# Layer 1 of a two-layer graph network in 880 groups of one chunk, with four tile numbers packed in a word

## The chip, the cores and the metric

The kernel runs on one core of one Trainium2 chip. The metric is the device time of one execution in microseconds (us); the lower the better. Each number of "before" is the median of three executions, or is read from one further execution that was taken with a profile.

## The reference, cut to what matters

There are 6250 nodes with 512 features, and 106,250 directed edges (50,000 drawn pairs in both directions and a self loop for each node), sorted by `dst`. Every layer sums over the edges of a node, divides by their number and multiplies by a weight matrix.

```python
def layer0(x, src, dst):                 # sums rows x[src] into node dst
    x_l = x @ W_l.T + b_l
    agg = segment_sum(x_l[src], dst, num_segments=6250)
    deg = segment_sum(ones, dst, num_segments=6250)
    return agg / maximum(deg, 1)[:, None] + x @ W_r.T

def layer1(h, src, dst):                 # sums rows h[dst] into node src
    neigh = segment_sum(h[dst] @ W_neigh.T + b_neigh, src, num_segments=6250)
    deg = segment_sum(ones, src, num_segments=6250)
    out = relu(h @ W_self.T + b_self + neigh / maximum(deg, 1)[:, None])
    return layernorm(h + out) * gamma + beta

x = layernorm(x + layer0(x, src, dst))
x = layernorm(x + layer1(x, src, dst))
```

## The kernel before

**Tiles, chunks, groups.** The 6250 nodes are T = 49 tiles of 128. An edge belongs to the tile of the node into which it is summed. The edges are laid out tile by tile in chunks of 128, one edge in each partition. A chunk is summed by TensorE: a gather brings the 128 table rows of its edges (1028 half-precision numbers each: high half, low half, scale), a 128x128 one-hot matrix says which node of the tile each edge goes to, and three matmuls multiply it with the high halves, the low halves and a column that counts edges. A group is a run of chunks of one tile whose matmuls accumulate in the same pair of PSUM banks. After a group, VectorE adds the 128x513 sum to `acc[:, tile, :]`. The number of groups is fixed from the worst case and not from the data, so groups that no tile needs stand at the end of the list. Positions to which no edge falls hold index 0 and a node offset that matches nothing.

**Layer 0** has 464 groups of two chunks, 928 chunks. In the same loop the edges of layer 1 are brought to their places: for each of 832 columns VectorE writes `where` (L901), a row of CHUNKS[1] positions, and TensorE multiplies it in two halves (`place`, L1178). `bin_starts` (L677) has worked out before it where each tile of a layer begins, and the tile of each group (`g_tile`, L720). It runs for layer 1 before the first table is written. Between the layers come the layer's weights and norm, 49 tiles long, in which the codes of layer 1's edges are unpacked (`decode_*`).

**Layer 1** has 464 groups of two chunks too. Its loop goes over 32 chunks at a time:

- POOL (`far_gathers`, L530) issues one indirect gather for each chunk into 16 buffers (`rows1`): eight in `rows`, five in `flat`, and one each in `g_loc`, `g_idx` and `edges`. For chunk n it waits until TensorE has done chunk n-16, and every eight chunks for the indices.
- ScalarE (`hots`, L1485) makes the one-hot matrices, four chunks at a time.
- TensorE (`row_sums`, L1262) sums the chunks into one of three pairs of PSUM banks, in the order `PAIR`, and waits until the addition that last used the pair is done. Beside the chunks it turns and multiplies one 128x512 block of h by `W_self` for every 16 chunks (`side_turn`, four transposes, and `side_product`, four fp32 matmuls), until all 49 blocks are done, after 800 chunks or so.
- VectorE (`adds`, L963) loads the group's tile number from `g_tile` into a register, waits for its own addition before, waits for the group's matmuls and adds (`add_group`, L952). It hands over indices and node offsets eight chunks at a time (`hand_batch`, L947), and for each block of h it adds two biases (`evict`, L910; `add_beta`, L915).
- SyncE moves the blocks of h and of the side products between DRAM and SBUF.

The lines of an addition are these:

```python
tile = dve.value_load(g_tile[1][0:1, ds(n, 1)], min_val=0, max_val=T - 1)
dve.wait_ge(s_acc, group0(1) + n)
dve.wait_ge(s_mm, chunk0(1) + G1 * (n + 1))
```

After the last addition come the inverse degrees and 49 tiles of projection and norms. All matmuls of a chunk have one line, 1117, since a helper issues them.

Of the kernel before, what the change touches and what calls it, by code (L numbers as in the profile page):

```python
# [18 lines left out]
def gnn_two_layers(nc, x, src, dst, w_l_t, b_l, w_r_t, w_self_t, b_self, w_neigh_t, b_neigh, gamma, beta, out):  # L19
    f32, f16, bf16, i32 = mybir.dt.float32, mybir.dt.float16, mybir.dt.bfloat16, mybir.dt.int32  # L20
    ALU, ACT, AX = mybir.AluOpType, mybir.ActivationFunctionType, mybir.AxisListType
    ds = bass.ds
# [3 lines left out]
    T = -(-N // P)  # L26
    LAST = N - (T - 1) * P
    KC = D // P
    U = 16
# [4 lines left out]

    GROUP = (2, 2)
    GROUPS = [-(-(-(-E // (P * g)) + T - 1) * g // U) * U // g for g in GROUP]

# [24 lines left out]
    with ctx:  # L62
# [69 lines left out]
        g_loc = [sb(f"g_loc{l}", [P, CHUNKS[l]], f32) for l in range(2)]  # L132
        g_tile = [sb(f"g_tile{l}", [1, CHUNKS[0]], i32) for l in range(2)]
        dst_next = g_idx[1][:, 0:EC]
        past = g_loc[1][0:T, :]
# [7 lines left out]
        row_unit = sb("row_unit", [P, 1], f32)  # L143
        PAIR = [0, 1, 2, 0, 1, 2, 0, 1]
        G1 = GROUP[1]
        assert len(PAIR) * G1 == U and CHUNKS[1] % (2 * U) == 0

# [316 lines left out]
        def _(pool):  # L464
# [34 lines left out]
            for layer in range(2):  # L499
# [29 lines left out]

                def far_gathers(i, first=False):  # L530
                    for k in range(2 * U):
                        n = 2 * U * i + k
                        if k % H == 0:
                            pool.wait_ge(s_idx, chunk0(1) // H + 2 * U // H * i + k // H + 1)
                        if not (first and k < U):
                            used = chunk0(1) + n - U + 1
                            if not isinstance(used, int):
                                used = pool.to_reg(used)
                            pool.wait_ge(s_sel, 2)
                            pool.wait_ge(s_mm, used)  # L540
                        nc.gpsimd.indirect_dma_start(  # L541
                            out=rows1[k % U], out_offset=None, in_=tables[1][:, :],
                            in_offset=bass.IndirectOffsetOnAxis(ap=idx_ring[:, k:k + 1], axis=0),
                        ).then_inc(s_row[k % U], 16)

                if layer == 0:
                    gathers(0, first=True)
                    with pool.Fori(1, CHUNKS[0] // U) as i:
                        gathers(i)
                else:  # L550
                    pool.wait_ge(s_mm, chunk0(1))
                    far_gathers(0, first=True)
                    with pool.Fori(1, CHUNKS[1] // (2 * U)) as i:
                        far_gathers(i)

            pool.wait_ge(s_deg, 2)
# [13 lines left out]
        def _(dve):  # L570
# [106 lines left out]
            def bin_starts(layer):  # L677
# [25 lines left out]
                for b in range(MB):  # L703
# [3 lines left out]
                dve.wait_ge(s["cscp"], 1)  # L707
                V.tensor_scalar(past, iota_chunk[0:T, :], cs_col[:, 0:1], None, ALU.is_ge).then_inc(s["past"], 1)
                link(V.tensor_scalar(base[:], cs_col[:], float(P * g), None, ALU.mult))
# [10 lines left out]
                V.tensor_copy(g_tile[layer][:, 0:n].rearrange("p (h c) -> p h c", h=2),  # L720
                              ps[0:1, 6:8, 0:half]).then_inc(s["list"], 1)

            def bin_rank(layer, b):
# [227 lines left out]

            def add_group(i, q):  # L952

                n = 2 * len(PAIR) * i + q
                tile = dve.value_load(g_tile[1][0:1, ds(n, 1)], min_val=0, max_val=T - 1)
                dve.wait_ge(s_acc, group0(1) + n)
# [6 lines left out]
            def adds(i, last=False, side=(None, None), beside=(None, None)):  # L963

                for q in range(2 * len(PAIR)):
                    b = G1 * q // H
                    if G1 * q % H == 0 and not (last and b >= 2):
                        hand_batch(2 * U // H * i + b + 2, (b + 2) % 4)
                    if q % len(PAIR) == 2 and beside[q // len(PAIR)] is not None:
                        add_beta(beside[q // len(PAIR)])  # L970
                    if q % len(PAIR) == len(PAIR) - 1 and side[q // len(PAIR)] is not None:
                        evict(side[q // len(PAIR)])
                    add_group(i, q)

            for layer in range(2):
# [14 lines left out]
                else:  # L990
# [8 lines left out]
                    adds(T // 2, side=(T - 2, T - 1), beside=(T - 1, None))  # L999
                    with dve.Fori(T // 2 + 1, iters // 2 - 1) as i:  # L1000
                        adds(i)
                    adds(iters // 2 - 1, last=True)
                dve.wait_ge(s_acc, group0(layer) + GROUPS[layer])
# [111 lines left out]
        def _(pe):  # L1115
# [145 lines left out]

            def row_sums(i, first=False, turn=(None, None), product=(None, None)):  # L1262
                for r in range(2):
                    for k in range(U):
# [19 lines left out]
            for layer in range(2):  # L1284
# [13 lines left out]
                else:  # L1298
# [6 lines left out]
                    with pe.Fori(T // 2 + 1, iters // 2) as i:  # L1305
                        row_sums(i)
                pe.wait_ge(s_acc, group0(layer) + GROUPS[layer])
                if layer == 1:
# [52 lines left out]
        def _(act):  # L1361
# [122 lines left out]

            def hots(i, first=False, turn=(None, None)):  # L1485
                for j in range(2 * U // HB):
                    n, at = 2 * U * i + HB * j, HB * (j % 2)
# [19 lines left out]
            with act.Fori(T // 2 + 1, CHUNKS[1] // (2 * U)) as i:  # L1507
                hots(i)
            act.wait_ge(s_lproj, 2 * T)

# [68 lines left out]
```

## Time and profile before

| | before |
|---|---|
| median of 3 executions | 3032.01 us (3031.95 to 3041.6) |
| profiled execution | 3039.64 us, its span 3037.9 us |
| from the first gather of layer 1 to its last addition's end | 1616.8 to 2808.0 us of the span |
| busy share of the span: TensorE, VectorE, ScalarE, POOL | 78%, 65%, 47%, 66% |
| mean granted TensorE clock | 0.907 of full speed |

The profiled execution is 7.6 us above the median and like the slowest of the three. Register, branch, semaphore and DMA-issuing instructions don't count as busy; an engine that is idle in the profile can be held by them.

### The profile page before, as it was taken

The page shows a single profiled execution, that of the slowest core. Times are in us where ns is not written, and L with a number is a line of the kernel's source. Part 1 is how long each engine was busy: PE and PEld are TensorE (multiplying, and loading weights), DVE is VectorE, ACT ScalarE, POOL GpSimd, SP SyncE. Part 2 cuts the span into 40 slices and gives each one's busy share as a digit, 9 for nine tenths or more (in the row PEclk, how much of TensorE's full clock was granted, in tenths as well). Part 3 has the DMA queues.
Part 4 walks back from the last instruction along what each step waited for, and adds up shares of the span by engine and source line. Part 5 has one row for each costly group of instructions (what it writes and reads, how often), then busy time and mean ns, then how long its engine had stood idle before and what let it go on. Part 6 is the DMA issues. An engine that isn't in the chain of part 4 may idle for free.

```text
span 3037.9 us, 52213 instructions
## 1 busy us (share of the span) xinstructions
PE 2376.5 (78%) x10032; PEld 1021.4 (34%) x10032; DVE 1960.0 (65%) x4549; ACT 1421.2 (47%) x3617; POOL 1998.1 (66%) x2069
## 2 busy tenths in 40 slices
PE   3288989989999988987885677776767777666996
PEld 2133434444444434433432232222323222221443
DVE  6899888888888888877873333333333333322898
ACT  3502555555565555553444443444344433431676
POOL 0276777777777777761115777777777777774785
PEclk8589999999999999999997989899888899865998
DMA  5577777777788777774557888888888888778676
GB/s 197 174 198 229 230 221 232 222 234 233 227 234 232 228 229 234 219 208 125 166 166 232 250 250 251 252 245 248 247 246 250 250 246 251 224 204 153 226 241 203
DMA packets 250848, 676.72 MB, mean 223 GB/s; under 512 B 40360, under 2 KB 41190, under 8 KB 250788
## 3 DMA queue, kind: packets, MB, share of 16 engines
q0 software_dynamic: 148480, 488.56, 57.0%
q1 hardware_dynamic: 101828, 186.19, 18.3%
q10 hardware_dynamic: 480, 1.28, 0.1%
q8 instruction: 24, 0.39, 0.1%
q14 instruction: 36, 0.29, 0.0%
HBM read 585.90 MB, written 89.97 MB: 222 GB/s over the span
## 4 chain that ended last, share of the span: by engine, by line
PE 32%; DMA 26%; DVE 17%; issue 14%; POOL 6%; DVEq 3%; ACT 1%; POOLq 1%; SPq 0%; ACTq 0%
PE ps L1117 31%; DMA rows<-table,idx_ring 13%; DMA flat<-table,idx_ring 9%; POOL rows L541 3%; DVE acc L889 2%; DVE onehot L876 2%; DVEq L883 2%; DMA table<-rows 1%; DVE where L901 1%; DMA edges<-table,idx_ring 1%; POOL flat L541 1%; POOL rows L525 1%; DVE flat L1072 1%; DVE spot L1072 1%; DVE flat L1089 1%
## 5 line engine op out<-in xcount | busy, mean ns | idle before, releaser
L1117 PE MATMUL ps<-rows,onehot 128*128 128x512 f16 x4176 | 895.3, 332 | 348.0 <-DMA rows<-table,idx_ring 172.3
L525 POOL DMA_INDIRECT rows<-table,idx_ring x928 | 895.1, 965 | 313.5 <-issue 207.5
L961 DVE TENSOR_TENSOR acc<-acc,ps 128x513 f32 x464 | 320.1, 690 | 798.2 <-PE ps L1117 795.5
L1117 PEld LDWEIGHTS ps<-rows,onehot 128*128 128x128 bf16 x4176 | 374.7, 102 | 919.3 <-issue 194.7
L541 POOL DMA_INDIRECT rows<-table,idx_ring x464 | 438.5, 945 | 158.5 <-issue 99.9
L1117 PE MATMUL ps<-where,put 128*128 128x464 bf16 x1664 | 467.9, 363 | 36.7 <-DVE where L901 28.2
L1117 PE MATMUL ps<-w_b,flat 128*128 128x512 f32 x784 | 463.4, 675 | 0.0
L901 DVE TENSOR_SCALAR where<-iota_chunk,cw_ring 128x928 bf16<-128x928 f16 x832 | 438.0, 526 | 7.5 <-PE ps L1117 0.6
L1425 ACT ACTIVATE put<-spot,flat 128x128 f16<-128x128 f16 x832 | 265.7, 390 | 338.1 <-PE ps L1117 330.7
L1413 ACT ACTIVATE spot<-iota_node,flat 128x128 f16<-128x128 f16 x832 | 340.4, 479 | 128.4 <-DVE flat L745 128.4
L889 DVE TENSOR_TENSOR acc<-acc,ps 128x513 f32 x464 | 318.1, 686 | 95.3 <-PE ps L1117 49.8
L541 POOL DMA_INDIRECT flat<-table,idx_ring x290 | 279.7, 964 | 88.3 <-issue 59.4
L876 DVE TENSOR_SCALAR onehot<-iota_node,loc_ring,rows 128x128 bf16<-128x128 f16 x928 | 311.1, 335 | 22.1 <-DMA rows<-table,idx_ring 20.4
L1493 ACT ACTIVATE apart<-iota_node,loc_ring 128x128 f16<-128x128 f16 x928 | 293.2, 387 | 6.2 <-DVE idx_ring L950 6.0
L1117 PE MATMUL ps<-w_a,flat 128*128 128x512 f32 x592 | 277.0, 612 | 5.4 <-ACT flat L1515 5.3
L1117 PE MATMUL ps<-flat,put 128*128 128x512 f16 (+1 forms) x870 | 195.1, 347 | 105.5 <-DMA flat<-table,idx_ring 95.3
L1498 ACT ACTIVATE onehot<-apart,row_unit 128x512 bf16<-128x512 f16 x116 | 83.7, 722 | 317.3 <-PE ps L1117 316.6
L1117 PEld LDWEIGHTS ps<-where,put 128*128 128x128 f16 x1664 | 121.0, 98 | 233.5 <-issue 104.2
L1117 PEld LDWEIGHTS ps<-flat,put 128*128 128x128 bf16 x870 | 77.4, 105 | 292.1 <-issue 151.9
L506 POOL COPY acc<-zeros 128x513 f32 (+1 forms) x49 | 35.2, 717 | 212.7 <-ACT flat L1450 212.7
L1483 ACT ACTIVATE flat<-ps 128x512 f32<-128x512 f32 x49 | 29.2, 597 | 306.7 <-PE ps L1117 306.7
L1117 PEld LDWEIGHTS ps<-w_a,flat 128*128 128x128 f32 x592 | 109.5, 195 | 122.3 <-issue 110.5
(233 smaller groups left out, 2450.2 us busy)
## 6 DMA issues: line engine op xcount, KB each, us to landing
table<-rows SPq DMA_DIRECT2D x98, 257.0 KB, 4.0
rows<-table,idx_ring POOLq DMA_INDIRECT x1392, 3.8
xr_scratch<-edges SPq DMA_DIRECT2D x49, 256.0 KB
rows<-xr_scratch SPq DMA_DIRECT2D x49, 256.0 KB, 3.2
h_scratch<-rows SPq DMA_DIRECT2D x49, 256.0 KB, 2.1
flat<-h_scratch SPq DMA_DIRECT2D x49, 256.0 KB
hb_scratch<-spot SPq DMA_DIRECT2D x49, 256.0 KB, 3.8
u_scratch<-flat SPq DMA_DIRECT2D x49, 256.0 KB
```

The source lines that it names most:

```text
L525: nc.gpsimd.indirect_dma_start(out=rows[:, k % GB, :], out_offset=None, in_=tables[layer][:, :], in_offset=bass.IndirectOffsetOnAxis(ap=id ...
L541: nc.gpsimd.indirect_dma_start(out=rows1[k % U], out_offset=None, in_=tables[1][:, :], in_offset=bass.IndirectOffsetOnAxis(ap=idx_ring[:, ...
L876: V.tensor_scalar(onehot[:, k % SB, :], iota_node[:], loc_ring[:, k:k + 1], rows[:, k % GB, 2 * D:2 * D + 2].bitcast(f32), ALU.is_equal, A ...
L883: tile = dve.value_load(g_tile[layer][0:1, ds(U // g * i + q, 1)], min_val=0, max_val=T - 1)
L889: V.tensor_tensor(tile_acc, tile_acc, part, ALU.add).then_inc(s_acc, 1)
L901: V.tensor_scalar(where_bf[:, k % PB, 0:CHUNKS[1]], iota_chunk[:, 0:CHUNKS[1]], cw_ring[:, k, 0:1], cw_ring[:, k, 1:2], ALU.is_equal, ALU. ...
L961: V.tensor_tensor(tile_acc, tile_acc, part, ALU.add).then_inc(s_acc, 1)
L1117: return nc.tensor.matmul(*args, skip_group_check=True, **kw)
L1413: last = nc.scalar.activation(spot[:, PB * g + k, :], iota_node[:], ACT.Abs, scale=value[:, ds(col + k, 1)], bias=shift_v[:, ds(col + k, 1)])
L1425: nc.scalar.activation((put1, put2)[g][:, k, :], spot[:, PB * g + k, :], ACT.Relu, scale=-1.0, bias=value[:, ds(col + k, 1)]).then_inc(s[" ...
L1493: last = nc.scalar.activation(apart[:, at + k, :], iota_node[:], ACT.Abs, bias=loc_ring[:, HB * j + k:HB * j + k + 1])
L1498: nc.scalar.activation(hot1[j % (U // HB)], apart[:, at:at + HB, :], ACT.Relu, bias=row_unit[:], scale=-2.0 ** -HS).then_inc(s_hot, HB)
```

## The change

Layer 1 is cut in 880 groups of one chunk (`GROUP = (2, 1)`), 880 chunks in place of 928. Layer 0 keeps its 464 groups of two. Since 880 is an odd number of 16s, every loop over 32 chunks gets a last half of 16. The order of the PSUM pairs is written out for 16 groups; it brings a pair back after three groups, and twice in 16 after two. The tile number isn't loaded for each addition: after the list of tile numbers is made, three further operations on one partition pack four 6-bit numbers in a word (`g_tiles`), VectorE loads a word for four additions, before the last addition of the four before, and splits it in registers. All that is as wide as layer 1's list becomes narrower: `where`, `past`, `place`, `decode_*`.

```diff
-    GROUP = (2, 2)
+    GROUP = (2, 1)
+        g_tiles = sb("g_tiles", [1, CHUNKS[1] // 4], i32)
-        PAIR = [0, 1, 2, 0, 1, 2, 0, 1]
+        PAIR = [0, 1, 2, 0, 1, 2, 0, 1, 2, 0, 1, 2, 0, 1, 2, 1]
-                def far_gathers(i, first=False):
-                    for k in range(2 * U):
+                def far_gathers(i, first=False, count=2 * U):
+                    for k in range(count):
...
+                    far_gathers(CHUNKS[1] // (2 * U), count=U)
...
+                if layer:
+                    dve.wait_ge(s["list"], 1)
+                    of = g_tile[1][:, 0:n].rearrange("p (c g) -> p c g", g=4)
+                    link(V.scalar_tensor_tensor(of[:, :, 0], of[:, :, 1], 64.0, of[:, :, 0], ALU.mult, ALU.add))
+                    link(V.scalar_tensor_tensor(of[:, :, 2], of[:, :, 3], 64.0, of[:, :, 2], ALU.mult, ALU.add))
+                    link(V.scalar_tensor_tensor(g_tiles[:], of[:, :, 2], 4096.0, of[:, :, 0], ALU.mult, ALU.add))
...
-            def add_group(i, q):
+            def four_tiles(i, q):
+
+                four = dve.value_load(g_tiles[0:1, ds(len(PAIR) // 2 * i + q // 4, 1)])
+                tiles = []
+                for k in range(4):
+                    one = dve.scalar_reg_alu(ALU.arith_shift_right, four, 6 * k) if k else four
+                    tiles.append(dve.snap(dve.scalar_reg_alu(ALU.bitwise_and, one, 63)).with_bounds(min_val=0, max_val=T - 1))
+                return tiles
+
+            def add_group(i, q, tile):
 
                 n = 2 * len(PAIR) * i + q
-                tile = dve.value_load(g_tile[1][0:1, ds(n, 1)], min_val=0, max_val=T - 1)
...
-                for q in range(2 * len(PAIR)):
+                count = len(PAIR) if last else 2 * len(PAIR)
+                following = four_tiles(i, 0)
+                for q in range(count):
...
-                    add_group(i, q)
+                    if q % 4 == 0:
+                        tiles = following
+                    if q % 4 == 3 and q + 1 < count:
+                        following = four_tiles(i, q + 1)
+                    add_group(i, q, tiles[q % 4])
```

## Rows read from the trace of the kernel before

**Rows 1.** The page: busy tenths of POOL, granted clock, GB/s, in 40 slices.
```profile
POOL 0276777777777777761115777777777777774785
PEclk8589999999999999999997989899888899865998
GB/s 197 174 198 229 230 221 232 222 234 233 227 234 232 228 229 234 219 208 125 166 166 232 250 250 251 252 245 248 247 246 250 250 246 251 224 204 153 226 241 203
```
**Rows 2.** Windows: busy (x instructions) PE, PEld, DVE, ACT, POOL; clock, DMA, GB/s.
```profile
1900.00:2200.00 300.00, 216.10 (x890) 86.70 (x889) 103.56 (x208) 120.05 (x310) 227.51 (x239) 0.91 0.83 248
...
2700.00:2720.00 20.00, 13.27 (x50) 4.18 (x49) 5.83 (x12) 7.78 (x20) 15.13 (x17) 0.73 0.75 210
...
2760.00:2780.00 20.00, 12.35 (x37) 3.38 (x36) 4.35 (x8) 5.78 (x15) 14.81 (x17) 0.50 0.97 158
```
**Rows 3.** Source line 541, layer 1's gathers: duration ns min/median/max, first and last start.
```profile
L541 POOL DMA_INDIRECT rows<-table,idx_ring x464: 942/946/967, 1616.8 to 2770.8; - x155
...
L541 POOL DMA_INDIRECT edges<-table,idx_ring x58: 942/946/948, 1635.6 to 2781.6; - x58
...
DMA to landing us min/median/max: 3.5/4.0/24.8
```
**Rows 4.** Timeline, the end of layer 1's edges: start, us, what, idle before.
```profile
2781.33 1.03 PE L1117 MATMUL ps<-rows,onehot 128*128 128x512 f16 x3 [0.55 <-DMA rows<-table,idx_ring]
...
2806.07 1.04 PE L1117 MATMUL ps<-edges,put 128*128 128x512 f16 x3 [0.21 <-DMA edges<-table,idx_ring]
...
2807.33 0.69 DVE L961 TENSOR_TENSOR acc<-acc,ps 128x513 f32 x1 [2.17 <-PE ps L1117]
```
**Rows 5.** Timeline of VectorE in layer 1, around a bias addition.
```profile
1646.44 0.69 DVE L961 TENSOR_TENSOR acc<-acc,ps 128x513 f32 x1 [1.64 <-PE ps L1117]
1647.05 0.69 DVE L919 TENSOR_TENSOR spot<-flat,edges 128x512 f32<-128x512 f32 x1
1647.65 0.69 DVE L961 TENSOR_TENSOR acc<-acc,ps 128x513 f32 x1
```
**Rows 6.** Waits, 400 to 1292 us: engine, line, waited for; us, times, longest.
```profile
DVE cw_ring L897 <- DVE idx_ring L853: 6.8, 38, 0.2
```
**Rows 7.** Source lines 955 and 961: the tile number's load and the addition; idle before.
```profile
L955 DVEq FUSED_REGOPS  x880: 53/190/190, 1611.5 to 2804.8; - x176
L955 DVEq TENSOR_LOAD <-g_tile x464: 299/305/970, 1611.0 to 2804.5; - x155
```
```profile
L961 DVEq FUSED_REGOPS  x464: 57/57/64, 1625.2 to 2807.2; - x155
L961 DVE TENSOR_TENSOR acc<-acc,ps x464: 679/690/692, 1625.3 to 2807.3; 128x513 f32 x155
...
  PE ps L1117: 795.5, 434
```
**Rows 8.** Timeline of TensorE in layer 1, at either clock.
```profile
2307.98 3.58 PE L1117 MATMUL ps<-rows,onehot 128*128 128x512 f16 x12 [1.37 <-DMA rows<-table,idx_ring]
...
2318.28 2.05 PE L1117 MATMUL ps<-w_b,flat 128*128 128x512 f32 x2
...
2321.74 1.10 PE L1117 MATMUL ps<-w_b,flat 128*128 128x512 f32 x2
...
2323.14 0.59 PE L1117 MATMUL ps<-g_loc,put 128*128 128x512 f16 x3
...
2323.60 0.59 PE L1117 MATMUL ps<-g_idx,put 128*128 128x512 f16 x3
```
**Rows 9.** Groups by form, 400 to 1292 us: busy us, mean ns; idle before, releasers.
```profile
L525 POOL DMA_INDIRECT rows<-table,idx_ring x692 | 669.1, 967 | 224.0 <-issue 145.5 <-PE ps L1117 78.5
...
L901 DVE TENSOR_SCALAR where<-iota_chunk,cw_ring 128x928 bf16<-128x928 f16 x691 | 363.7, 526 | 6.7 <-PE ps L1117 0.6
```
**Rows 10.** Timeline of VectorE where `g_tile` of layer 1 is written.
```profile
97.15 0.63 DVE L720 CAST g_tile<-ps 1x464 int32<-1x464 f32 x1
97.70 0.17 DVE L842 TENSOR_SCALAR top<-top 128x49 f32<-128x49 f32 x1
```

More of the change, by code:

```diff
@@ L143, in gnn_two_layers @@
         row_unit = sb("row_unit", [P, 1], f32)
-        PAIR = [0, 1, 2, 0, 1, 2, 0, 1]
+        PAIR = [0, 1, 2, 0, 1, 2, 0, 1, 2, 0, 1, 2, 0, 1, 2, 1]
         G1 = GROUP[1]
-        assert len(PAIR) * G1 == U and CHUNKS[1] % (2 * U) == 0
+        assert len(PAIR) * G1 == U and CHUNKS[1] % (2 * U) == U and CHUNKS[1] % HB == 0
         def pair_before(q):
@@ L707, in bin_starts @@
                 dve.wait_ge(s["cscp"], 1)
-                V.tensor_scalar(past, iota_chunk[0:T, :], cs_col[:, 0:1], None, ALU.is_ge).then_inc(s["past"], 1)
+                V.tensor_scalar(past, iota_chunk[0:T, 0:CHUNKS[1]], cs_col[:, 0:1], None, ALU.is_ge).then_inc(s["past"], 1)
                 link(V.tensor_scalar(base[:], cs_col[:], float(P * g), None, ALU.mult))
@@ L963, in adds @@
             def adds(i, last=False, side=(None, None), beside=(None, None)):
-                for q in range(2 * len(PAIR)):
+                count = len(PAIR) if last else 2 * len(PAIR)
+                following = four_tiles(i, 0)
+                for q in range(count):
                     b = G1 * q // H
-                    if G1 * q % H == 0 and not (last and b >= 2):
+                    if G1 * q % H == 0 and not last:
                         hand_batch(2 * U // H * i + b + 2, (b + 2) % 4)
@@ L999, in _ @@
                     adds(T // 2, side=(T - 2, T - 1), beside=(T - 1, None))
-                    with dve.Fori(T // 2 + 1, iters // 2 - 1) as i:
+                    with dve.Fori(T // 2 + 1, iters // 2) as i:
                         adds(i)
-                    adds(iters // 2 - 1, last=True)
+                    adds(iters // 2, last=True)
                 dve.wait_ge(s_acc, group0(layer) + GROUPS[layer])
@@ L1260, in sums, with row_sums @@
                         x_turn(turn, half)
-            def row_sums(i, first=False, turn=(None, None), product=(None, None)):
-                for r in range(2):
+            def row_sums(i, first=False, turn=(None, None), product=(None, None), halves=2):
+                for r in range(halves):
                     for k in range(U):
@@ L1306, in _ @@
                         row_sums(i)
+                    row_sums(iters // 2, halves=1)
                 pe.wait_ge(s_acc, group0(layer) + GROUPS[layer])
@@ L1483, in side_turned, with hots @@
                 nc.scalar.activation(h_t, ps[:, 0, :], ACT.Copy).then_inc(s_ltc, 1)
-            def hots(i, first=False, turn=(None, None)):
-                for j in range(2 * U // HB):
+            def hots(i, first=False, turn=(None, None), count=2 * U):
+                for j in range(count // HB):
                     n, at = 2 * U * i + HB * j, HB * (j % 2)
@@ L1508, in _ @@
                 hots(i)
+            hots(CHUNKS[1] // (2 * U), count=U)
             act.wait_ge(s_lproj, 2 * T)
```

## The prediction

> **What bounds the kernel now.** I read the page first, by its slices. POOL is at 7 tenths in two long stretches, one for each layer's edges, and GB/s falls from about 250 to 204 and 153 at the end of the second [rows 1]. So I asked for windows of that stretch. Between 1900 and 2200 us POOL issues 239 gathers in 300 us, one each 1.255 us, at 248 GB/s, with VectorE busy 104 of 300 us and TensorE 216 [rows 2]. The source view of the gathers gives the same pace over nearly the whole stage: chunk 0 starts at 1616.8 and chunk 919, the last in `rows`, at 2770.8, so (2770.8 - 1616.8) / 919 = 1.2557 us per chunk; a gather lasts 0.946 us of it and the other 0.31 is POOL's own issue [rows 3]. VectorE's idle time before its additions is 795.5 us, 434 times for the matmuls [rows 7]: it follows. The stage is therefore POOL's instruction count times 1.2557 us, up to a point.
>
> That point shows in the last rows. After about 2720 us POOL goes on at its pace, but 210 GB/s become 158 while the DMA engines' share rises from 0.75 to 0.97 [rows 2], and the time to landing, 4.0 us in the median, ends at 24.8 us [rows 3]. TensorE then takes a chunk when its rows land: 15 chunks from 2781.33 to 2806.07 are 24.74 / 15 = 1.65 us each, and the last addition starts at 2807.33 and ends at 2808.0 [rows 4]. What is special there? I counted the edge list of the reference: with ceilings per tile, groups of 256 edges need 440 groups, that is 880 chunks. Chunk 880 is issued at 1616.8 + 880 x 1.2557 = 2721.8 us, where the rate falls. The 48 chunks behind it are padding; every lane has index 0, so all 128 rows are the same table row. I take it that they are slow because of that; the trace shows the time and place only.
>
> **The change, part by part.** Its time is summed against the profiled execution, 3039.6 us.
>
> *Fewer chunks in layer 1.* With groups of 128 the same count gives 854 chunks with edges, and 880 in all, so 26 of padding. Chunks with edges: 880 - 854 = 26 fewer at POOL's 1.2557 us, -32.6 us. Padding: 48 - 26 = 22 fewer at 1.65 us, -36.3 us. Together -68.9. This supposes that POOL stays what paces the stage, so the rest is whether VectorE and TensorE keep below 16 x 1.2557 = 20.1 us in 16 chunks.
>
> *VectorE.* It has 16 additions in 16 chunks where it had 8. One is 0.690 us [rows 7]. Each waits for the one before. How long from its end to the next one's start, when all else is ready? No addition in the trace shows it well. The nearest row is a copy that waits for its predecessor, then for a second semaphore, then has its register operations: 6.8 us in 38 times, 0.18 us [rows 6]; the upper bound I take is 0.25, the same with a 0.057 us register step more [rows 7]. So 16 x 0.87 = 13.9 us (15.0 at most). A bias addition behind an addition delays the next one by little: three starts 0.61 and 0.60 us apart [rows 5], against 0.87 without it, so 2 x 0.35 = 0.7 (2 x 0.75 at most). Handing over, 0.3 to 0.5. Splitting a word happens four times: the load is 0.305 us, the register work for its address up to 0.190, and seven shifts and masks with four copies cost between one fused step at 0.190 and eleven at 0.057, 0.63 [rows 7]; with gaps 0.8 to 1.3 us. It is issued while the addition before runs, which covers 0.69. So 0.1 to 0.6 is exposed, and all 1.3 if nothing is covered; I take 0.4, in all 1.6. The sum is 13.9 + 0.7 + 0.4 + 1.6 = 16.6 us of 20.1, and the upper bound 15.0 + 1.5 + 0.5 + 5.2 = 22.2. The two are far apart; I take the lower because row 5 shows an addition starting 0.6 us behind another operation with its whole load of a tile number between them, so register work is indeed covered.
>
> *TensorE.* At the high clock a chunk is 0.46 us (2323.14 to 2323.60) and at the low one 3.58 / 4 = 0.895; a side matmul is 1.10 or 2.05 [rows 8]. With four of these in 16 chunks that is 7.4 + 4.4 = 11.8 us or 14.3 + 8.2 = 22.5. At the present mean clock of 0.91 [rows 2], 18% of the time at the low level, it is about 13.7 of 20.1. Its waits for additions change: a pair of banks held two chunks, now one, so it can be three chunks ahead of VectorE and not six. A chunk needs the addition three before: 0.87 + 0.87 us lie between, more than a chunk at either clock, and less than a side matmul and a chunk at the low one (2.95). The 16 gather buffers stand between such stalls and POOL: a row lands after some 5 chunks, which leaves about 11, or 13 us. I add 4 us for stalls that come through (0 to 18).
>
> *Do more additions slow POOL?* In layer 0 a gather has a mean of 0.967 us beside a busy VectorE, in layer 1 a median of 0.946 [rows 3, 9]. If the denser additions did what layer 0's work does, it would be 880 x 0.021 = 18 us; I take 0, because the long ones stand out in the layer that has `where`, and an addition reads PSUM in both. The Trainium skill, "SBUF — State Buffer", section "SBUF: two separate sides", says the same of the mechanism: only an operation in a two-port mode keeps GpSimd from writing descriptors, and a later section there says that `tensor_tensor` has no such mode. By that rule the term is 0, by the bound from layer 0 it is +18.
>
> *Layer 0.* `where` is 928 wide at 0.526 us [rows 9] and becomes 880: 5% less, 0.027 x 832 = 22 us of VectorE, and the `place` matmuls lose as much on TensorE. But POOL paces this stage too. Of its 224.0 us idle before 692 gathers, 692 x 0.30 = 208 is issue, so 16 us are real waits, and 15 more are in gathers over 0.946 [rows 9]; over 832 columns 37 us is all that there is to win. A 5% lighter load removes a part: I take -4 (0 to -20).
>
> *Before the first gather.* The copy to `g_tile` has 880 elements for 464, 0.63 us becomes about 1.05 [rows 10], and three small linked operations on 220 elements of one partition come behind it, about 0.33 each by that row's slope and floor. The next operation started at once at 97.70 and all wait for it [rows 10], so +1.4 (0.8 to 2.5). The narrower `decode_*` give back 0.5.
>
> Sum: -68.9 - 4 + 4 + 1.4 - 0.5 = -68. So 3039.6 becomes 2971.6 in a like execution, and the median, which is 7.6 lower, 2964.
>
> **Rivals.**
> *The tail is not the padding's.* If the slow end belongs to the end of the stage whatever stands there, 48 chunks fewer are worth POOL's pace only: -60.3, and the time is 2973. For it: I know the cause from the count alone. Against: the rate falls at the very chunk.
> *Additions do slow gathers.* +18: 2982.
> *Layer 0 gains more.* All 20 in place of 4: 2948.
> *VectorE becomes the bound.* At 22.2 us for 16 chunks, 1.39 per chunk, the stage is 880 x 1.39 = 1223 us against 2808 - 1617 = 1191 now, +32, less 3 elsewhere: 3061, slower. It decides when splitting a word costs more than (20.1 - 15.0) / 4 = 1.3 us exposed, or 1.0 with the upper prices of all else. Against it stands row 5; for it, that no row shows a split in registers.
> *TensorE loses its clock.* One-chunk groups at VectorE's pace break up the bursts in which it now works. At the low clock throughout the side work, 22.5 us in 16 chunks is 2.4 over POOL's pace, 50 times 120 us, less 68: 3084, slower. It costs nothing until the low level takes (20.1 - 11.8) / (22.5 - 11.8) = 78% of the time, a granted clock of 0.61; now it is 0.91, and 0.73 and 0.50 where the side work has ended [rows 2]. A lag fills the bursts again, which speaks against it. The Trainium skill, "TensorE: Matmul & The Clock Gate", section "A second HAM failure mode: psum-queue depth-cycling", describes a matmul kernel cycling through PSUM banks whose short idles between groups made the clock swing; by that rule the clock falls here. The falls behind 2700 us, where matmuls are sparse, agree with it; no row shows it beside side work.
>
> **How the numbers follow.** Chances: the forecast 0.60 (its own range 2955 to 2978), the tail 0.10, additions against gathers 0.07, layer 0 0.06, VectorE 0.07, the clock 0.10, half of it as a part of the price that ends at 2980 to 3020. The first four lie in 2945 to 2985 with 0.83; for my unknown prices on VectorE, of which a part would add some 20 us, I set 2940 to 3000. A measurement of this kernel tells 0.3%, 9 us. Faster by more: 0.60 + 0.10 + 0.07 + 0.06 and some 0.03 of partial prices, 0.86. Within 9 us: 0.04. Slower: 0.10.
>
> **What the profile after would show.** 880 gathers at L541, first start near 1618, pace 1.256 us, POOL's idle 0.30 as before. The fall of GB/s 854 chunks later, near 2690, and the last addition near 2740. 880 additions of 0.69 us, spaced 0.87 to 0.95 where rows are in store, with a longer one each fourth; VectorE busy near 0.6 of the stage. A granted clock above 0.8 between 1900 and 2200. `where` near 0.50 us. I am wrong if POOL's idle before its gathers grows above 0.30 with TensorE named: then the pace is VectorE's or the clock's, and the waits of TensorE say which.

## The result, and the profile after

| | before | after |
|---|---|---|
| median of 4 executions | 3032.91 us (3031.95 to 3041.6) | 2964.87 us (2956.62 to 2966.32) |
| span of the profiled execution | 3037.9 us | 2962.5 us |
| layer 1's edges, first gather to end of the last addition | 1191.2 us | 1124.2 us |
| VectorE busy, share of the span | 65% | 76% |

The ratio is 0.9764, with a 95% interval of 0.9738 to 0.9789: 2.4% faster, where 2964 us had been forecast. Of the 75.4 us between the two spans 67.0 lie in the stage that the change is about, 6.4 before it and 2.0 behind it.

The source view of layer 1's gathers, which answers to [rows 3]: duration min/median/max in ns, first and last start, then what ended POOL's idle time.

```profile
L542 POOL DMA_INDIRECT rows<-table,idx_ring x440: 945/949/1469, 1610.4 to 2707.6; - x147
...
L542 POOL DMA_INDIRECT edges<-table,idx_ring x55: 945/949/950, 1629.3 to 2717.6; - x55
its engine sat idle before it (us, times) until:
  issue: 186.9, 613
  PE ps L1139: 72.0, 236
...
DMA to landing us min/median/max: 3.5/3.9/14.7
```

Chunk 871 starts at 2707.6, so the pace is 1097.2 / 871 = 1.260 us; before it was 1.256. The difference is the median duration of a gather, 0.949 us for 0.946. The idle times are 0.305 us each, by whichever name (186.9 / 613, 72.0 / 236): what POOL takes anyway. It never waits for the additions, of which there are twice as many. The longest landing is 14.7 us where it was 24.8: 26 chunks of padding stand at the end where there were 48.

Windows, which answer to [rows 2]: busy us (x instructions) of PE, PEld, DVE, ACT, POOL; granted clock, DMA share, GB/s.

```profile
1900.00:2200.00 300.00, 222.42 (x895) 89.84 (x894) 187.98 (x330) 123.60 (x315) 227.45 (x239) 0.87 0.83 248
...
2660.00:2680.00 20.00, 14.62 (x48) 4.18 (x48) 11.66 (x21) 7.78 (x20) 15.15 (x16) 0.63 0.74 211
2680.00:2700.00 20.00, 13.85 (x42) 3.80 (x42) 9.92 (x18) 5.89 (x15) 15.19 (x16) 0.54 0.79 183
2700.00:2720.00 20.00, 11.73 (x35) 3.40 (x36) 8.29 (x12) 2.61 (x6) 14.21 (x15) 0.50 0.92 159
```

VectorE is busy 188 of 300 us where it was 104, POOL as long as before, and the clock is 0.87 for 0.91. The fall from 211 to 159 GB/s has moved: chunk 854 is issued at 1610.4 + 854 x 1.260 = 2686, in the window that shows 183.

The source view of the additions, for [rows 7]:

```profile
L977 DVEq ALU_OP  x1540: 40/45/51, 1618.0 to 2733.7; - x193
L977 DVEq FUSED_REGOPS  x880: 57/57/57, 1618.1 to 2733.8; - x176
L977 DVE TENSOR_TENSOR acc<-acc,ps x880: 674/690/693, 1618.2 to 2733.9; 128x513 f32 x176
...
  PE ps L1139: 301.1, 387
  DVE acc L977: 130.5, 358
```

358 times the addition before is what an addition waited for, 0.36 us after its end. The timeline of VectorE shows it where rows are in store:

```profile
2316.82 0.69 DVE L977 TENSOR_TENSOR acc<-acc,ps 128x513 f32 x1 [0.31 <-PE ps L1139]
2317.89 0.69 DVE L977 TENSOR_TENSOR acc<-acc,ps 128x513 f32 x1 [0.38 <-DVE acc L977]
2318.96 0.69 DVE L977 TENSOR_TENSOR acc<-acc,ps 128x513 f32 x1 [0.38 <-DVE acc L977]
2319.57 0.68 DVE L921 TENSOR_TENSOR flat<-ps,where 128x512 f32<-128x512 f32 x1
2320.17 0.68 DVE L977 TENSOR_TENSOR acc<-acc,ps 128x513 f32 x1
```

Additions start 1.00 or 1.07 us apart. Of four tile numbers in a word three need a shift and a mask, two of the 45 ns register operations above, and the first needs the mask alone: that makes the 1540, 7 for each word. 1.00 is the distance of one addition in four and 1.07 that of the other three, which fits. The word for the next four is loaded before the last addition of a word, and that one is no later than the two before it, so the load is covered.

### The profile page after: what moved, and what is told of

Its sections match the earlier page's. It is cut to its first block, busy times and chain, and to the rows that moved or that the text cites. A ratio compares the mean times of both kernels' runs of the same rounds, so it can differ in the third digit from the quotient of the medians.

```text
span 2962.5 us, 53780 instructions
## 1 busy us (share of the span) xinstructions
PE 2333.3 (79%) x9888; PEld 1014.9 (34%) x9888; DVE 2242.3 (76%) x4956; ACT 1402.1 (47%) x3557; POOL 1953.1 (66%) x2021
## 4 chain that ended last, share of the span: by engine, by line
PE 37%; DVE 19%; DMA 19%; issue 13%; POOL 5%; DVEq 4%; ACT 1%; POOLq 0%; SPq 0%; ACTq 0%
PE ps L1139 36%; DMA rows<-table,idx_ring 16%; POOL rows L542 4%; DVE acc L897 3%; DVE acc L977 3%; DVE onehot L884 2%; DVEq L891 2%; DVE where L909 2%; POOL rows L526 1%; DMA table<-rows 1%; DMA g_idx<-table,idx_ring 1%; DVE flat L1094 1%; DVE flat L1047 1%; DVE st L1051 1%; DVE flat L1049 1%
## 5 line engine op out<-in xcount | busy, mean ns | idle before, releaser
L1139 PE MATMUL ps<-rows,onehot 128*128 128x512 f16 (+1 forms) x4104 | 896.3, 335 | 365.8 <-DMA rows<-table,idx_ring 172.9
L526 POOL DMA_INDIRECT rows<-table,idx_ring x928 | 894.4, 964 | 309.3 <-issue 211.8
L977 DVE TENSOR_TENSOR acc<-acc,ps 128x513 f32 x880 | 606.4, 689 | 440.9 <-PE ps L1139 301.1
L542 POOL DMA_INDIRECT rows<-table,idx_ring x440 | 422.9, 961 | 150.5 <-issue 95.4
L1139 PE MATMUL ps<-where,put 128*128 128x440 bf16 x1664 | 451.0, 353 | 37.9 <-DVE where L909 36.6
L1139 PE MATMUL ps<-w_b,flat 128*128 128x512 f32 x784 | 470.1, 684 | 0.0
L909 DVE TENSOR_SCALAR where<-iota_chunk,cw_ring 128x880 bf16<-128x880 f16 x832 | 428.1, 515 | 8.6 <-PE ps L1139 1.7
L897 DVE TENSOR_TENSOR acc<-acc,ps 128x513 f32 x464 | 318.3, 686 | 97.1 <-PE ps L1139 55.1
L542 POOL DMA_INDIRECT flat<-table,idx_ring x275 | 260.7, 948 | 83.8 <-issue 61.6
L1516 ACT ACTIVATE apart<-iota_node,loc_ring 128x128 f16<-128x128 f16 x880 | 278.6, 388 | 54.3 <-DVE idx_ring L958 54.3
L1139 PE MATMUL ps<-flat,put 128*128 128x512 f16 (+1 forms) x825 | 160.7, 322 | 18.4 <-DMA flat<-table,idx_ring 13.0
L1139 PEld LDWEIGHTS ps<-w_b,flat 128*128 128x128 f32 x784 | 129.9, 208 | 54.6 <-issue 13.0
```

Of the source, the lines that this page charges most:

```text
L526: nc.gpsimd.indirect_dma_start(out=rows[:, k % GB, :], out_offset=None, in_=tables[layer][:, :], in_offset=bass.IndirectOffsetOnAxis(ap=id ...
L542: nc.gpsimd.indirect_dma_start(out=rows1[k % U], out_offset=None, in_=tables[1][:, :], in_offset=bass.IndirectOffsetOnAxis(ap=idx_ring[:, ...
L897: V.tensor_tensor(tile_acc, tile_acc, part, ALU.add).then_inc(s_acc, 1)
L909: V.tensor_scalar(where_bf[:, k % PB, 0:CHUNKS[1]], iota_chunk[:, 0:CHUNKS[1]], cw_ring[:, k, 0:1], cw_ring[:, k, 1:2], ALU.is_equal, ALU. ...
L977: V.tensor_tensor(tile_acc, tile_acc, part, ALU.add).then_inc(s_acc, 1)
L1139: return nc.tensor.matmul(*args, skip_group_check=True, **kw)
```

## The experiments

Each ratio is to the kernel before on the same chip. "Stage" is the time from layer 1's first gather to the end of its last addition, read from the profiled execution of each kernel. The kernel before had a median of 3025.2 to 3026.2 us beside all of them but row_3000.

### What the padding costs

```diff
# spread_after, spread_before, spread_after2: lane[p] = 48 * p
-                link(V.tensor_tensor(g_idx[1][:], code_b, code_a, ALU.add))
+                link(V.tensor_tensor(code_b, code_b, code_a, ALU.add))
+                link(V.tensor_scalar(code_a, raw, 0.0, lane[:, 0:1], ALU.is_equal, ALU.mult))
+                link(V.tensor_tensor(g_idx[1][:], code_b, code_a, ALU.add))
# ones_912
+    GROUPS[1] = 912
```

> The changed kernel, with the index of every empty position set to 48 times its partition number in place of 0, by one wider step and one more operation in the unpacking of the codes, so that padding gathers 128 different table rows. Theory of the prediction (padding chunks are slow, 1.65 us each, because all lanes read one row): the 26 chunks of padding at the end go at POOL's pace of 1.26 us and the rows land some 5 us after their issue; layer 1's edges end 10 to 16 us earlier and the time falls from 2965 to about 2952; GB/s stays near 210 to the end. Rival (the end of the stage is slow whatever the indices are, for instance because TensorE's clock has fallen or because many transfers are queued): no change, 2965, and GB/s falls to 158 as before.

> The kernel before, with the same edit of the indices of empty positions. Theory: 48 chunks of padding gain 0.4 us each and the backlog of about 20 us at the last landing goes: 19 to 22 us less than 3033, about 3012. With it the change (880 chunks for 928) would be worth only POOL's pace, 48 x 1.256 = 60 us, on kernels that have no slow padding. Rival: no change, 3033.

> The changed kernel with 912 groups of one chunk in place of 880: the same 854 chunks with edges, 58 of padding for 26. Theory: 32 more chunks of padding at 1.65 us are 53 us, and layer 0's wider place work gives back about 3, so 3020. Rival (a chunk more costs POOL's pace whatever it holds): 32 x 1.26 = 40 us, 3007.

| kernel | chunks + padding at the end | stage, us | ratio (interval) |
|---|---|---|---|
| spread_after | 854 + 26, spread | 1110.4 | 0.9734 (0.9709 to 0.9758) |
| spread_before | 880 + 48, spread | 1168.7 | 0.9941 (0.9923 to 0.9960) |
| ones_912 | 854 + 58, row 0 | 1174.4 | 0.9956 (0.9942 to 0.9971) |

All three came out as the theory had it. For spread_after it is the stage and the windows that say so: 9 us of its median is about the width of the interval. The windows of spread_after cover the same end of the stage:

```profile
2660.00:2680.00 20.00, 16.47 (x49) 4.48 (x48) 11.63 (x21) 8.49 (x23) 15.12 (x17) 0.50 0.77 210
2680.00:2700.00 20.00, 16.65 (x50) 4.57 (x49) 11.33 (x19) 7.06 (x18) 15.13 (x17) 0.50 0.73 212
```

and those of ones_912, with 58 chunks that read row 0:

```profile
2680.00:2700.00 20.00, 12.57 (x38) 3.40 (x37) 8.58 (x14) 5.78 (x15) 15.13 (x16) 0.50 0.87 158
2700.00:2720.00 20.00, 12.50 (x37) 3.37 (x36) 8.60 (x16) 5.88 (x15) 15.14 (x16) 0.50 0.89 159
```

TensorE's clock is 0.50 in both, POOL is as busy in both; the rate differs with the indices alone. With the indices spread, 212 GB/s hold to the end, the longest landing is 6.7 us, and the kernel before gains 22.5 us of stage (1191.2 to 1168.7). From after_again below (1120.7) to ones_912, 32 chunks of padding cost 53.7 us, 1.68 each.

The counts say one thing more. In the kernel before, 880 chunks stand ahead of the padding, but the edges fill 854: 26 tiles end in a group whose second chunk is empty and reads row 0 in all lanes, as the padding does. These empty chunks lie one by one among full ones, and POOL's pace and the rate hold over them (248 GB/s in [rows 2]). All 48 chunks that the change removes hold no edge, 26 of them there and 22 at the end.

### Whether packing the tile numbers is needed

```diff
# load_each; the three packing operations and four_tiles are gone
-                    add_group(i, q, tiles[q % 4])
+                    add_group(i, q, dve.value_load(g_tile[1][0:1, ds(2 * len(PAIR) * i + q, 1)], min_val=0, max_val=T - 1))
```

> The changed kernel without the packed words: each addition loads its own tile number, as before the change, and the three packing operations are gone. The trace after shows 0.31 to 0.38 us between additions and a pace of 16.8 us and more for 16 additions. Theory: the load and its register work (0.305 and about 0.45 us) are issued while the addition before runs and stay covered, or add up to 0.1 to 0.2 us each; 16 x 1.2 is still under POOL's 20.1, so no change, 2964 within 6. Rival: the load goes past its cover by 0.3 us or more each, 16 x 1.37 and the bias additions pass 20.1 us, VectorE paces the stage and the time is 3000 or more.

Ratio 0.9750 (0.9726 to 0.9774), stage 1118.4: as fast as the changed kernel. The theory held. VectorE in load_each:

```profile
2307.09 0.69 DVE L971 TENSOR_TENSOR acc<-acc,ps 128x513 f32 x1 [0.32 <-DVE acc L971]
2308.11 0.69 DVE L971 TENSOR_TENSOR acc<-acc,ps 128x513 f32 x1 [0.33 <-DVE acc L971]
2309.12 0.69 DVE L971 TENSOR_TENSOR acc<-acc,ps 128x513 f32 x1 [0.33 <-DVE acc L971]
```

With a load for each, additions are 1.01 us apart, less than the 1.07 of the changed kernel. A load of 0.303 us and its register work (two steps of up to 0.190) don't lengthen that, so they run while the addition before runs. Which part of the gap of 0.32 us is the wait and which the 0.057 us register step behind it isn't shown: the changed kernel's first addition of a word has a mask of 45 ns more there and is no further away, 1.00.

### What the rest of the change did

```diff
# wide_both, layer 0's loop alone
-                V.tensor_scalar(where_bf[:, k % PB, 0:CHUNKS[1]], iota_chunk[:, 0:CHUNKS[1]], cw_ring[:, k, 0:1],
+                V.tensor_scalar(where_bf[:, k % PB, 0:CHUNKS[0]], iota_chunk[:, 0:CHUNKS[0]], cw_ring[:, k, 0:1],
-                        last = mm(ps[:, 2 * n + b, 0:half], put[:, k % PB, :],
+                        last = mm(ps[:, 2 * n + b, 0:CHUNKS[0] // 2], put[:, k % PB, :],
-                                  (where_bf if layer else where)[:, k % PB, b * half:(b + 1) * half], start=start, stop=stop)
+                                  (where_bf if layer else where)[:, k % PB, b * half:b * half + CHUNKS[0] // 2], start=start, stop=stop)
```

> The changed kernel once more, unchanged, as the mark for the others of this set. Its ratio to the kernel before should be 0.976 within 0.003. In the profiles so far the first gather of layer 1 starts anywhere from 1598 to 1617 us, in kernels that do the same before it, so the 6.4 us that the changed kernel was ahead there in its first profile are not known to be the change's.

> The changed kernel with layer 0's place work as wide as before the change: where is written 928 wide in place of 880, and each of its two matmuls streams 464 columns in place of 440. Only layer 0's loop is touched. Theory of the prediction: POOL paces layer 0 as well and the narrower work gave 4 us (0 to 20) through fewer real waits, so this kernel takes 2 to 6 us more than the changed one, most of it before layer 1's first gather. Rival (layer 0 is paced by TensorE and VectorE, whose 1664 matmuls get 10 ns longer each and whose 832 operations 25 ns): 17 to 20 us more.

after_again: 0.9771 (0.9742 to 0.9801), stage 1120.7. wide_both: 0.9761 (0.9734 to 0.9788), stage 1119.9. The wide place work costs nothing that can be measured, and a gain of 17 to 20 us is excluded. Layer 0's gathers take from 1187.1 to 1202.3 us, first to last start, in the three kernels with 464 columns to a matmul (before, wide_both, spread_before) and from 1188.6 to 1197.0 in the nine with 440 (without row_3000, whose chip was slower): means of 1195.3 and 1191.5. That agrees with 4 us and doesn't show them; the shortest of all is ones_912 with 456 columns, 1185.9.

### How far the stage is from VectorE's and TensorE's limit

```diff
# dve_more
                 V.tensor_tensor(tile_acc, tile_acc, part, ALU.add).then_inc(s_acc, 1)
+                V.tensor_tensor(spare[:, q % 2, :], zeros[:, 0:D], zeros[:, 0:D], ALU.add)
# two_pairs
-        PAIR = [0, 1, 2, 0, 1, 2, 0, 1, 2, 0, 1, 2, 0, 1, 2, 1]
+        PAIR = [0, 1] * 8
-                        if k % G1 == 0 and not (first and r == 0 and q < 3):
+                        if k % G1 == 0 and not (first and r == 0 and q < 2):
```

> The changed kernel with one further VectorE operation behind each of layer 1's 880 additions, 512 wide, from two SBUF operands, whose result nobody reads. By the trace after, additions are 1.00 to 1.07 us apart when nothing else is missing; with a further operation they should be 1.21 apart (starts 0.61 and 0.60 after each other), so 16 chunks take 19.4 us, the bias additions 1.2 and handing over 0.3: 20.9, against POOL's 20.1. Theory (VectorE has a margin of 20% in the changed kernel, and the 16 gather buffers absorb the rest): VectorE paces the stage by little, 0.05 us per chunk, 40 us more: 3000. Rival (the margin is as wide as the prediction's sum of 16.6 us had it, so that the operation fits): no change within 6 us. Second rival (VectorE and TensorE take turns, three chunks apart, and are near their limit together): 100 us more.

> The changed kernel with two pairs of PSUM banks in turn for layer 1's sums in place of three, so that a chunk's matmuls wait for the addition two before. At the high clock a chunk of 0.46 us and its hand-over fit beside an addition's 1.05 us, at the low one 1.04 do barely, and a side matmul in front of a chunk does not. Theory (POOL paces the stage and 16 gather buffers hide what VectorE and TensorE lose to each other): 0 to 10 us more. Rival (the third pair is what keeps the one-chunk groups under POOL's pace): 40 us more or above.

dve_more: 0.9872 (0.9841 to 0.9903), stage 1148.1, that is 27 us more than after_again. The timeline has additions 1.20 us apart and no idle time:

```profile
2300.16 0.67 DVE L978 TENSOR_TENSOR acc<-acc,ps 128x513 f32 x1
2300.76 0.67 DVE L979 TENSOR_TENSOR spare<-zeros 128x512 bf16<-128x512 f32 x1
2301.36 0.67 DVE L978 TENSOR_TENSOR acc<-acc,ps 128x513 f32 x1
```

and its windows a VectorE that is never idle, with POOL's gathers down to 232 in 300 us:

```profile
1900.00:2200.00 300.00, 224.20 (x877) 93.37 (x876) 300.00 (x552) 119.53 (x304) 229.59 (x232) 0.83 0.80 243
```

So the threshold is where the sum put it: about 20.7 us of VectorE for 16 chunks is just over POOL's 20.1. The expected 40 us were 27 to 31. The 0.6 us operation costs so little because additions come 1.20 us apart in place of 1.00 or 1.07: most of it falls in the gap in which VectorE waits for its own addition, and the rest had the margin under POOL's pace.

How POOL is held to that pace is not by waiting for buffers. Its idle time before a gather is 0.305 us here too (174.2 us in 572, 92.3 in 303), and it stays six chunks ahead of the additions from chunk 16 to chunk 832, where the buffers would allow 16. What has grown is the gathers themselves: 151 of 880 last longer than 0.96 us, at the same places of each 16 chunks, and all that is over 0.946 in them is 34.0 us, where the first profile after has 27 of them and 5.7 us. The 28 us between are about what the stage is longer. One such place, VectorE and POOL together:

```profile
2005.59 0.68 DVE L979 TENSOR_TENSOR spare<-zeros 128x512 bf16<-128x512 f32 x1
2006.19 0.68 DVE L928 TENSOR_TENSOR spot<-flat,edges 128x512 f32<-128x512 f32 x1
2006.20 1.49 POOL L543 DMA_INDIRECT flat<-table,idx_ring  x1 [0.30 <-PE ps L1141]
```

and one of the changed kernel:

```profile
2080.90 0.68 DVE L927 TENSOR_TENSOR spot<-flat,edges 128x512 f32<-128x512 f32 x1
2081.24 1.17 POOL L542 DMA_INDIRECT rows<-table,idx_ring  x1 [0.30 <-issue]
```

A gather that starts while VectorE runs a large operation with both operands in SBUF lasts longer, by what is left of that operation less some 0.15 us. In the twelve profiles without the further operation and without row_3000, 233 gathers of layer 1 last over 0.98 us, and during every one of them the bias addition `spot<-flat,edges` runs (L927 here, L919 before), the only VectorE operation of the stage with two large SBUF operands. The more of it is left when the gather starts, the longer the gather, from 1.02 us with 0.2 us left to 1.47 with nearly all of its 0.68. Gathers that start during an addition to `acc`, which reads PSUM, don't grow. dve_more adds 880 operations of that kind and has 148 gathers over 0.98 us, where after_again has 19; no run takes the bias additions out.

So dve_more adds, beside its 0.6 us, an operation that itself holds gathers up. Its loss is not a clean measure of VectorE's margin; that VectorE is never idle in its window is what shows that the margin is used up.

two_pairs: 0.9779 (0.9746 to 0.9812), stage 1121.0, as after_again. TensorE waits more for additions, and the 16 gather buffers hide it:

```profile
  PEld ps L1139: 466.3, 618
```

These are its waits for additions before a weight load, us and times; the changed kernel has 363.2 in 338.

### Which sharing of a row is slow

```diff
# own_row: 7 * chunk for all lanes; row_3000: 3000 for all padding
+                link(V.scalar_tensor_tensor(code_a, raw, 0.0, iota_chunk[:, 0:CHUNKS[1]], ALU.is_equal, ALU.mult))
+                link(V.tensor_scalar(code_a, code_a, 7.0, None, ALU.mult))
# row_3000
+                link(V.tensor_scalar(code_a, raw, 0.0, 3000.0, ALU.is_equal, ALU.mult))
```

> The changed kernel, with the index of every empty position set to 7 times its chunk's number: all 128 lanes of a padding chunk read one table row, but each chunk another one. The first kernels of this study showed that 128 different rows take the slow end away. Theory (the lanes of one gather hold each other up): padding is as slow as with row 0, 1.6 to 1.65 us a chunk, near 158 GB/s, and the time is that of the changed kernel, ratio 0.977 to the kernel before. Rival (what is slow is that gathers of many chunks, all in flight, read row 0): the end goes at POOL's pace near 210 GB/s, ratio 0.973.

own_row: 0.9752 (0.9729 to 0.9775), stage 1111.6, 9 us less than after_again. Its window at the end of the stage:

```profile
2680.00:2700.00 20.00, 14.13 (x46) 4.19 (x47) 10.84 (x18) 6.50 (x16) 15.13 (x17) 0.60 0.76 211
```

The theory that was put first fell: 128 lanes may read one row at POOL's pace, if the next chunk reads another. The ratio alone couldn't tell the two theories apart, since its interval holds both 0.973 and 0.977; the window and the stage do.

> The changed kernel, with the index of every empty position set to 3000: all padding reads one table row, as in the changed kernel, but not the table's first. With a row of its own for each chunk the slow end was gone, so lanes of one gather may share a row. Theory (the row that all gathers in flight share is slow, whichever it is): layer 1's edges take 1120 us as in the changed kernel, GB/s falls to 158 after chunk 854, ratio 0.977. Rival (row 0 is special by its place in the table): 1110 us, 210 GB/s to the end, ratio 0.973 to 0.975.

Its time is inconclusive: ratio 0.9881 (0.9849 to 0.9912). The chip on which it ran took 3506.9 us for the kernel before and 3463.6 for this one, with gaps of 2 to 3 us in POOL's and VectorE's queues throughout, so POOL did not keep its pace and no stage can be compared. Its windows, one ahead of the padding, whose 26 gathers start from 3186.8 on, and two near the end:

```profile
3100.00:3120.00 20.00, 14.61 (x49) 5.56 (x50) 10.65 (x19) 6.58 (x18) 13.29 (x15) 0.76 0.69 195
3180.00:3200.00 20.00, 10.20 (x35) 3.11 (x36) 8.91 (x16) 5.78 (x15) 11.56 (x13) 0.70 0.81 150
3200.00:3220.00 20.00, 12.67 (x47) 4.06 (x45) 11.17 (x20) 7.78 (x20) 13.06 (x15) 0.70 1.02 143
```

With 15 gathers issued in 20 us in the first window and in the last, 195 GB/s come through ahead of the padding and 143 in it, and the DMA engines are busier for fewer bytes, as where row 0 is shared (0.97 at 158 GB/s in [rows 2]) and not as in own_row (0.76 at 211). So sharing a row other than the first slows the queue too, by this one profile; no kernel with row 0 was profiled on that chip, and how much of it is the chip's isn't known.

### Both edits together

> The changed kernel with both edits that seemed to gain: empty positions read 48 times their partition's number, and each addition loads its own tile number, without the packed words and the 2.3 us that making them takes before the first gather. Sum of parts: 14 us from layer 1's end and 2 to 3 us from the missing packing, so ratio 0.9715 to 0.973; if packing is worth what its cover of the load suggests, 0.974.

> The changed kernel with the spread indices alone, once more and in more rounds, as the mark for the kernel that also drops the packing: ratio 0.972 to 0.974 to the kernel before, layer 1's edges in 1110 us.

spread_each: 0.9733 (0.9709 to 0.9757), 2942.79 us, stage 1107.5. spread_after2: 0.9741 (0.9719 to 0.9764), 2949.89 us, stage 1108.4. Both lie below the changed kernel's 0.9764 and 0.9771, by about the width of the uncertainty, and both stages lie below its two by 12 us and more. Between themselves they don't differ by more than is uncertain. The fastest version found is therefore the changed kernel with spread indices, and it doesn't need the packed words.

## Why the prediction was right, step by step

- **POOL paces the stage, and its price is a count.** Right. The cleanest measure is between kernels without slow padding: 880 + 48 chunks take 1168.7 us, 854 + 26 take 1110.4, 1108.4 and 1107.5, mean 1108.8. The difference is 59.9 us for 48 chunks, 1.248 each, against POOL's 1.2557.
- **What the 48 chunks were.** Put a little wrong, without effect: I called 26 of them chunks with edges, but by my own count they held none. They ran at POOL's pace all the same, as priced.
- **Padding at 1.65 us.** Right (1.68 from after_again to ones_912), and the first rival, a tail that is not the padding's, fell. Stage against stage the forecast was -68.9 + 4 = -64.9; measured -67.0, and -70.5 with after_again. What is over the pace comes out as 22.5 us in the kernel before (to spread_before) and 11.9 in the changed one (1120.7 to 1108.8): 10.6 less, where 22 x (1.65 - 1.256) = 8.7 had been counted in.
- **VectorE stays below 20.1 us in 16 chunks.** Right in its verdict, mis-sized in its term. I took 0.18 us (0.25 at most) between the end of an addition and the next, from a copy of another kind; it is 0.31 or 0.38, and 0.32 with a load each, outside my bound. Sixteen additions take 12 x 1.07 + 4 x 1.00 = 16.8 us, where I had 13.9. Against that, a bias addition adds 0.14 (1.21 for 1.07) and not 0.35, and the splitting, put at 0.4 us exposed four times, shows in the 12 x 0.07 us that are already counted and nowhere else. With 0.3 for two bias additions and 0.3 for handing over it is about 17.4, where I had 16.6: the errors partly cancelled, and that is luck. An error of 3 us more would have passed 20.1, the pace at which dve_more loses time. A slip beside it: the exposed split that decides with all upper prices is (20.1 - 17.0) / 4 = 0.8 us, not 1.0.
- **The four us for stalls.** None came through: POOL's idle time before a gather stays at 0.305 us. No row showed such a stall; the term offset the -4 of layer 0, so the sum didn't show it. Even two pairs of banks in turn bring no stall to POOL.
- **More additions don't slow gathers.** Right: the median is 0.949 us in the first profile after and 0.946 in the others with 880 additions, as before. The 18 us of the bound are excluded for additions that read PSUM, and the rule of the Trainium skill's page "SBUF — State Buffer", by which the term is 0, agrees with that. As I took it, for `tensor_tensor` of any kind, it is too wide: the bias additions are `tensor_tensor` too, with both operands in SBUF, and they do lengthen the gathers that start beside them, by 5.7 us in all in the first profile after and 5.5 in the one before. The term is 0 because that number didn't change, and because `acc` is added to from PSUM.
- **Layer 0, -4 us.** Neither shown nor refuted. `where` went from 0.526 to 0.515 us in the mean and not to 0.50, so the 22 us of VectorE were 9, and `place` has 440 columns, but layer 0's length moves by more than 4 us from kernel to kernel. The 6.4 us by which the changed kernel reached its first gather earlier are within that scatter: 1598 to 1617 us over all kernels.
- **Before the first gather, +1.4 us.** It is +2.3: from the start of the copy to the start of what follows is 2.83 us now, 0.55 in [rows 10]. The packing operations take 0.54 us each where I had 0.33:

```profile
97.47 1.06 DVE L722 CAST g_tile<-ps 1x880 int32<-1x880 f32 x1
98.57 0.54 DVE L727 SCALAR_TENSOR_TENSOR g_tile<-g_tile 1x220 int32<-1x220 int32 x1
...
100.30 0.19 DVE L850 TENSOR_SCALAR top<-top 128x49 f32<-128x49 f32 x1
```

- **The clock.** Right in its verdict: it stayed far above the 0.61 from which it would have cost time. Its fall from 0.91 to 0.87, between 1900 and 2200 us, is in the direction that the Trainium skill's "TensorE: Matmul & The Clock Gate" (section "A second HAM failure mode: psum-queue depth-cycling") lets expect of a kernel that cycles through PSUM banks with short idles, but the other profiles don't bear it out as the change's: in the same window spread_before has 0.90 with two-chunk groups, own_row and ones_912 have 0.90 with one-chunk groups, and two_pairs has 0.91. One-chunk groups are worth 0.04 at most and perhaps nothing.
- The exact hit of the median is luck in part: the spans differ by 75.4 us, the interval of the ratio is 15 us wide, and two terms without a measured effect, +4 and -4, cancelled.

## What to carry to other kernels

When an engine issues one fixed-price instruction for each unit of work, price a change by the count of units, and check that the other engines stay below that pace per unit; here doubling VectorE's additions was free. Look at what fills a worst-case count: 48 empty units in a row cost more each than full ones, and giving them harmless, different addresses was worth 12 us of the stage in the changed kernel and 22 in the one before (9 and 18 by the ratios). A register load in front of an operation cost nothing while the engine was busy with the one before; trading the loads for shifts gained no time and put additions 0.06 us further apart.

## What the runs showed of the hardware that I had not expected

- Indirect gathers of 128 rows of 2056 bytes run at 158 GB/s, 1.65 us each, when the gathers in flight all read row 0, and hold 211 GB/s and POOL's pace when each gather reads one row of its own in all lanes, or 128 different rows. The rate falls with what queued gathers share, not with what the lanes of one share. Row 3000 in place of row 0 slowed them too, 143 GB/s where 195 had come through, on one chip that was slow throughout; how far that holds stays open.
- A gather that POOL issues while VectorE runs a `tensor_tensor` of 128x512 from two SBUF operands lasts up to 1.4 to 1.5 us in place of 0.946; a `tensor_tensor` that reads one operand from PSUM leaves it at 0.946.
- A wait of VectorE for its own preceding addition, with a second wait and a register step for the address behind it, leaves 0.31 to 0.38 us between the two; without a wait the next operation starts 0.60 us after the start of the one before, inside its 0.69.
- The start of layer 1's gathers varied by 19 us (1598.2 to 1617) among profiles of kernels whose work before it is nearly the same (row_3000 left out). Gains of a few us in the first half of this kernel can't be read from single profiles.
